# A pipelined transformer layer with eight experts: choice of experts behind the fourth transpose on VectorE, rank products behind the values, slot arithmetic on GpSimd, v ahead of q, the sums' transposes ahead of the next chunk

## What is computed

```
# block 0: base product + low-rank product (8 x 16 ranks, mixed by cond_8), then an fp8 product
u  = x @ W_base.T + b_base + 2 * sum_e cond_8[b,e] * (x @ As[e].T) @ Bs[e].T
x  = x + (fp8(bf16(u) / s_in) @ fp8(kernel / s_k)) * s_in * s_k + bias8
# block 1: z = x mixed by a weight of each sequence, then pre-norm attention, then one expert per token
z  = x @ (sum_g cond_8[b,g] * weight[g] * mask).T + bias
hn = layernorm(z);  q, k, v = hn @ wq + bq, hn @ wk + bk, hn @ wv + bv     # 16 heads of 8
z  = z + softmax(q k' / sqrt(8)) v @ wo + bo
hn2 = layernorm(z); idx = argmax(hn2 @ gate_w + gate_b)                    # 8 experts
x  = x + z + relu(hn2 @ w1[idx] + b1[idx]) @ w2[idx] + b2[idx]
```

## Time and profile before

| | us |
|---|---|
| median of 3 timed runs | 330.72 (330.45, 333.46, 330.72) |
| the profiled execution, its own time | 328.03 |
| span of the profiled execution | 326.2 |
| PE busy in the span | 257.6 (79%) |
| DVE busy | 211.4 (65%) |
| ACT busy | 194.9 (60%) |
| POOL busy | 198.3 (61%) |

### The profile page before, as it was taken

How to read it: one execution, slowest core, us unless ns; L and a number is a source line. 1 busy time by engine, 2 the same in 40 slices (tenths; PEclk the granted TensorE clock), 3 DMA queues, 4 the chain that set the end, 5 groups by cost and what they waited for, 6 DMA issues and landing times.

```text
span 326.2 us, 10489 instructions
## 1 busy us (share of the span) xinstructions
PE 257.6 (79%) x3558; PEld 197.4 (61%) x3565; DVE 211.4 (65%) x588; ACT 194.9 (60%) x422; POOL 198.3 (61%) x270
## 2 busy tenths in 40 slices
PE   3786979989799798798767574875994898999970
PEld 1454646756567567566554362354984787999970
DVE  4923698997979989889879558234252644656530
ACT  1578596986968969868837423033742344666640
POOL 1250572887887778866865538612866355787760
PEclk9999999999999999999795855559998799999995
DMA  6261101002010037010100100571532434333300
GB/s 211 99 219 73 34 3 34 3 34 67 3 67 32 0 113 324 32 36 2 46 24 2 67 3 0 138 222 49 155 110 79 128 103 120 89 97 90 96 22 0
DMA packets 13195, 24.65 MB, mean 76 GB/s; under 512 B 2636, under 2 KB 8784, under 8 KB 12896
## 3 DMA queue, kind: packets, MB, share of 16 engines
q1 hardware_dynamic: 9792, 17.26, 17.2%
q0 software_dynamic: 2784, 6.32, 5.7%
q10 hardware_dynamic: 576, 0.53, 0.5%
HBM read 16.60 MB, written 7.95 MB: 75 GB/s over the span
## 4 chain that ended last, share of the span: by engine, by line
PE 49%; DVE 21%; issue 11%; ACT 8%; POOL 3%; another core or an unknown queue 3%; DMA 2%; DVEq 1%; SPq 1%; POOLq 0%; ACTq 0%
PE so L735 7%; PE d L418 6%; PE d L430 6%; PE so L418 5%; PE so L430 5%; DVE mx L1163 4%; DVE pt L1181 4%; PE d L787 3%; DMA pack_sb<-pack 2%; PE d L760 2%; PE so L722 2%; PE d L775 2%; PE d L706 2%; POOL rs L1346 2%
## 5 line engine op out<-in xcount | busy, mean ns | idle before, releaser
L639 POOL DMA_INDIRECT out<-ob,rin x39 | 39.3, 1007 | 24.8 <-DVE w1s L564 11.1
L1419 POOL DMA_INDIRECT routed<-rows,slot x32 | 33.1, 1035 | 10.1 <-issue 10.1
L706 PE MATMUL d<-ybd,pack_sb 128*128 128x256 f32 x112 | 29.8, 396 | 0.0
L1353 POOL TENSOR_TENSOR t<-pr 128x512 f32<-128x512 f32 x16 | 20.5, 1281 | 13.2 <-ACT pr L959 13.2
L735 PE MATMUL so<-pt,v 32*32 32x128 f32 x1024 | 20.0, 295 | 10.4 <-DVE pt L1181 9.0
L418 PE MATMUL d<-xt,w1s 128*128 128x128 f32 x160 | 23.8, 294 | 3.3 <-issue 1.9
L430 PE MATMUL d<-pack_sb,mid 128*128 x160 | 24.0, 297 | 2.9 <-ACT mid L460 2.8
L1174 DVE SCALAR_TENSOR_TENSOR acc<-so,pack_sb,acc 128x512 f32<-128x512 f32 x24 | 17.9, 746 | 12.8 <-ACT acc L1065 12.1
L418 PE MATMUL so<-xt,w1s 128*128 128x128 f32 x152 | 21.7, 282 | 5.1 <-DVE ob L577 3.8
L430 PEld LDWEIGHTS d<-pack_sb,mid 128*128 128x128 f32 x160 | 21.1, 205 | 5.2 <-issue 5.2
L959 ACT ACTIVATE pr<-pr 128x512 f32<-128x512 f32 x32 | 20.0, 624 | 6.8 <-DVE pr L1167 6.7
(11 more groups left out here) (184 smaller groups left out, 665.2 us busy)
## 6 DMA issues: line engine op xcount, KB each, us to landing
rin<-routed SPq DMA_DIRECT2D x39, 128.5 KB
pack_sb<-pack SPq DMA_DIRECT2D x1, 2576.0 KB, 9.2
w1s<-w SPq DMA_DIRECT2D x8, 322.0 KB, 3.4
xb<-x_t SPq DMA_DIRECT2D x8, 256.0 KB, 3.5
pack_sb<-pack SPq DMA_DIRECT2D x1, 2048.0 KB, 8.3
routed<-pad SPq DMA_DIRECT2D x5, 128.5 KB
out<-ob,rin POOLq DMA_INDIRECT x39
pack_sb<-pack SPq DMA_DIRECT2D x1, 584.0 KB, 6.0
```

The costliest lines, as they stand in the source:

```text
L639: pool.indirect_dma_start(out, bass.IndirectOffsetOnAxis(rin[s % 8][:, 2 * H:ROW].bitcast(U32), 0), ob[u][:, :], None, bounds_check=N_TOK ...
L706: mm = pe.matmul(mix_bank(a, k)[:, u * 256:(u + 1) * 256], col[f"mix_w{k // 2}"][:, (blk % 4) * P:(blk % 4 + 1) * P], ybd[:, :, :].rearran ...
L1353: pool.tensor_tensor(t16[:, f, :], e32[:, :, 0:16], e32[:, :, 16:32], ALU.add).then_inc(sem["sums"], 1)
L1419: pool.indirect_dma_start(routed, bass.IndirectOffsetOnAxis(slot[:, g:g + 1], 0), rows[:, g, :], None).then_inc(sem["scattered"], 16)
```

## The change

It moves operations between places and engines and removes none of the results:

- DVE: in turns that have `j`, `pick` goes from between `shifted(2)` and `shifted(3)` to behind the fourth transpose, and `rank` from ahead of the fourth transpose to behind `eighth`.
- `place` leaves DVE. POOL does it with five small operations (a product, three adds of halves in place of one reduction, the cast) ahead of its scatters, with a semaphore `placed` of its own; `slot` now counts only the two operations of `rank`.
- POOL issues three of the four scatters, then `x1`, then the fourth.
- PE: the rank products go from ahead of wk to behind the values; wv, coded, wq in place of wq, coded, wv; the transposes of `rc` go ahead of `lora_a` of the next turn.
- ACT: `rc`, `v`, `qt`, then `yb`, `yb2` in place of `qt`, `rc`, `yb`, `yb2`, `v`.

```
@@ PE, start of a turn
+                if m is not None:
+                    wait(pe, "rcx", m + 1)
...
+                    for g in range(NG):
+                        mm = pe.transpose(turned_back(m)[:, g * P:(g + 1) * P],
+                                          rc[:, g * NH:(g + 1) * NH, :].rearrange("p h d -> p (h d)"), col["ident"])
+                    mm.then_inc(sem["rt_mm"], 1)
                 if a is not None:
                     wait_turn(pe, "x_in", a, p, 2)
                     wait(pe, "q_out", a - 1)
...
@@ PE, end of a turn
                     values(range(0, NG)).then_inc(sem["pv_mm"], 1)
...
+                if m is not None:
+                    wait(pe, "pick", 6 * (m + 1))
+                    pe.matmul(gates(m)[:, 64:64 + NG * E], upper_b[:, :], oh_b[:, :, :].rearrange("p g e -> p (g e)"),
+                              start=True, stop=False, skip_group_check=True)
...
+                    mm.then_inc(sem["rank_mm"], 1)
+                if late(m) and m == NC - 2:
+                    turn(0)
+                    hidden(0)
+                    turn(1)
                 if n is not None:
                     wait(pe, "x1_tok", n + 1)
...
+                if a is not None and not (isinstance(a, int) and a == 0):
+                    coded(a, n)
+                if n is not None:
+                    if m is not None:
+                        wait(pe, "slot", 2 * (m + 1))
+                    pe.matmul(dn[0][:, :], col["wq"], hn_t[:, :], start=True, stop=True).then_inc(sem["qkv_mm"], 1)
@@ ACT
-                if n is not None:
-                    wait(act, "qkv_mm", 3 * n + 2)
-                    act.activation(qt[:, :], dn[0][:, :], ACT.Identity, bias=col["bq"]).then_inc(sem["q_out"], 1)
                 if j is not None:
                     wait(act, "recip", j + 1)
...
+                if n is not None:
+                    wait(act, "qkv_mm", 3 * n + 2)
+                    wait(act, "pv_mm", n)
+                    act.activation(v[:, :, :], groups(dn[3][:, :]), ACT.Copy).then_inc(sem["v_out"], 1)
+                    wait(act, "qkv_mm", 3 * n + 3)
+                    act.activation(qt[:, :], dn[0][:, :], ACT.Identity, bias=col["bq"]).then_inc(sem["q_out"], 1)
@@ DVE
-                if m is not None:
+                if m is not None and j is None:
                     pick(m)
...
                     turned(j, 1)
                     turned(j, 2)
-                if m is not None:
-                    rank(m, p)
                 if j is not None:
                     turned(j, 3)
-                if m is not None:
-                    place(m)
+                if m is not None and j is not None:
+                    pick(m)
                 if early:
                     first_b()
                 if a is not None:
                     eighth(a)
                 if isinstance(a, int) and a == 1:
                     split_out_dve(dve)
+                if m is not None:
+                    rank(m, p)
@@ POOL
+            def place(m):
+                wait(pool, "slot", 2 * (m + 1))
+                hold(pool, "held_pool")
+                pool.tensor_tensor(pos[:, :, :], pos[:, :, :], oh_b[:, :, :], ALU.mult).then_inc(sem["placed"], 1)
...
+                pool.tensor_tensor(pos4[:, :, :], pos[:, :, 0:4], pos[:, :, 4:8], ALU.add).then_inc(sem["placed"], 1)
...
+                pool.tensor_tensor(pos2[:, :, :], pos4[:, :, 0:2], pos4[:, :, 2:4], ALU.add).then_inc(sem["placed"], 1)
...
+                pool.tensor_tensor(slot_f[:, :], pos2[:, :, 0], pos2[:, :, 1], ALU.add).then_inc(sem["placed"], 1)
...
+                pool.tensor_copy(slot[:, :], slot_f[:, :]).then_inc(sem["placed"], 1)
...
                 if m is not None:
+                    place(m)
                     wait(pool, "ids", m + 1)
                     wait(pool, "resid", m + 1)
-                    wait(pool, "slot", 5 * (m + 1))
+                    wait(pool, "placed", 5 * (m + 1))
                     wait(pool, "hn2", NG * (m + 1))
                     hold(pool, "held_pool")
-                    for g in range(NG):
...
+                    for g in range(NG - 1):
+                        scatter(g)
...
                     pool.tensor_tensor(x1[:, p, :], xb[:, p, :], yb2[:, :], ALU.add).then_inc(sem["x1"], 1)
+                if m is not None:
+                    scatter(NG - 1)
```

More of the change, by code:

```diff
@@ L877, in iteration @@
                     mm.then_inc(sem["hn_tr"], 1)
-                if m is not None:
-                    wait(pe, "pick", 6 * (m + 1))
-                    pe.matmul(gates(m)[:, 64:64 + NG * E], upper_b[:, :], oh_b[:, :, :].rearrange("p g e -> p (g e)"),
-                              start=True, stop=False, skip_group_check=True)
-                    for g in range(NG):
-                        mm = pe.matmul(gates(m)[:, 64 + (g + 1) * E:64 + (NG + 1) * E].rearrange("p (g e) -> p g e", e=E),
-                                       ones_b[:, :], oh_b[:, g, :].unsqueeze(1).to_broadcast([P, NG - g, E]),
-                                       start=False, stop=(g == NG - 1), skip_group_check=True)
-                    mm.then_inc(sem["rank_mm"], 1)
                 if late(m) and m == NC - 2:
@@ L910, in iteration @@
                     values(range(0, NG)).then_inc(sem["pv_mm"], 1)
-                    if late(m) and m == NC - 2:
-                        turn(0)
-                        hidden(0)
-                        turn(1)
-                if n is not None:
-                    if m is not None:
-                        wait(pe, "slot", 5 * m + 2)
-                    pe.matmul(dn[0][:, :], col["wq"], hn_t[:, :], start=True, stop=True).then_inc(sem["qkv_mm"], 1)
-                if a is not None and not (isinstance(a, int) and a == 0):
-                    coded(a, n)
+                if m is not None:
+                    wait(pe, "pick", 6 * (m + 1))
+                    pe.matmul(gates(m)[:, 64:64 + NG * E], upper_b[:, :], oh_b[:, :, :].rearrange("p g e -> p (g e)"),
+                              start=True, stop=False, skip_group_check=True)
+                    for g in range(NG):
+                        mm = pe.matmul(gates(m)[:, 64 + (g + 1) * E:64 + (NG + 1) * E].rearrange("p (g e) -> p g e", e=E),
+                                       ones_b[:, :], oh_b[:, g, :].unsqueeze(1).to_broadcast([P, NG - g, E]),
+                                       start=False, stop=(g == NG - 1), skip_group_check=True)
+                    mm.then_inc(sem["rank_mm"], 1)
[3 more added lines that the diff above has]
+                    turn(1)
                 if n is not None:
@@ L1080, in iteration @@
                     normed(1)
-                if n is not None:
-                    wait(act, "qkv_mm", 3 * n + 3)
-                    wait(act, "pv_mm", n)
-                    act.activation(v[:, :, :], groups(dn[3][:, :]), ACT.Copy).then_inc(sem["v_out"], 1)
             def between(act):
```

50 lines of the change are left out of this document (22 added, 28 removed).

## The result

The changed kernel takes **340.36 us** (median of 4 runs, 338.85 to 342.56) against 332.09 (4 runs, 330.45 to 333.81) of the kernel before beside it: a ratio of 1.0315, 95% interval 1.0255 to 1.0376. It is slower by 8.3 us, where +2.1 was forecast. The profiled execution took 341.0, span 339.2.

The account below looks back on a forecast made before the run. No engine is full; a turn is a ring of waits through several, ACT just behind DVE. Turn terms +1.0 +1.0 -0.4 +2.7 -0.3 -0.5 -1.4 gave +2.1 on a timed 330.72: 332.8 us, range 327.5 to 337.

Parts of the forecast that it names:

- The step that failed: POOL's list after the slots: three scatters, x1 in 1.11, fourth scatter 1.26, ybd 0.63, putting ybd at T' + 11.3.
- rival 1: Values' signal as late as 3.26, so slots at T' + 3.85 and 0.65 more per turn: 335.4 us; chance 0.25.
- Choice and rank off the path: DVE before the fourth transpose: 1.4 leaves the path, but ACT is next, so values gain only 0.43 a turn.
- The values' signal and `rank`: DVE behind the values: rank starts at T' + 2.9, slots there at T' + 3.2, bounds 2.75 and 3.85.
- lora_a: PE product waiting for ACT's qt behind rc and v: starts near T' + 6.0 instead of T + 4.14.
- POOL's arithmetic: Five dependent small operations making the slots on POOL: 1.45 in all, bounds 1.1 and 1.85.
- The mis-sized term: POOL between slots and first scatter: 0.17 of issue.
- Turns 1 to 3: Later qt costs +1.0 in turn 1 and +1.0 in turn 2; turn 3 gains 0.4.
- Turns 7 and 8: 1.4 taken off DVE counts: turn 7 -0.3; turn 8 -0.5, bounds +0.5 and -1.4.
- Turn 9: Values 2.5 sooner without pick's wait for the gate, then +1.1 behind them at half clock: sum -1.4.
- Rival 3: Shorter gaps in turns 8 and 9 keep PE at 2.4 GHz, saving up to 6: 326.8 us; chance 0.12.
- Rivals 2 and 4: POOL keeps its cover, signal early: 330.4, chance 0.15; choice brings whole 1.4 in seven turns: 321, chance 0.06.

Follow-up runs that it names:

- e13: The changed kernel unaltered, run again against the kernel before: 340.18 us, ratio 1.022.
- e14: The changed kernel with the 2.6 MB load also waiting until the scatters have landed, against the kernel before: 332.82 us, ratio of medians 1.003.
- e6: The kernel before with v ahead of q on PE and ACT and rc ahead of both, nothing else: 338.07 us, ratio 1.021.
- e4: The kernel before with only the slots' arithmetic moved from DVE to POOL, all four scatters ahead of x1: 330.03 us, ratio 1.027.
- e5: The kernel before with only the choice and rank products moved, slots' arithmetic staying on DVE behind rank: 332.20 us, ratio 0.997.
- e12: The kernel before unaltered, run against itself and profiled: 331.95 us, ratio 1.002.
- e9: The kernel before with the choice behind the fourth transpose in turn 9 alone: 318.43 us, ratio 0.997.
- e15: The kernel before with choice, v-first order and rc transposes moved, slots' arithmetic on DVE, four scatters ahead of x1: 333.85 us, ratio 1.004.
- e7: The kernel before with only the transposes of rc moved ahead of lora_a: 334.66 us, ratio 1.005.
- e16: The kernel before unaltered, run against itself once more: 331.83 us, ratio 0.992.
- e2: The kernel before with only the fourth scatter put behind x1: 326.71 us, ratio 1.017.
- e10: The kernel before with choice moved, place on DVE, fourth scatter behind x1, and the 2.6 MB load waiting for scatters: 329.25 us, ratio 1.026.
- e8: The kernel before with the choice behind the fourth transpose in turns 8 and 9 only: 319.79 us, ratio 1.001.

## Why the prediction was wrong, point by point

**The step that failed** is the one that went through POOL's list and moved the fourth scatter behind `x1`. I priced that scatter at 1.26 on POOL's own queue and went on to `ybd`. I did not ask who waits for its landing (ACT's `rows`, for the buffer) nor what `x1` releases besides PE (SP's load). "Three scatters, x1, the fourth" read as a gain of 1.26 for `x1`; it also sends a scatter through the DMA engines together with 2576 KB, once. No rival had it. It costs 7.4 us (e13 against e14) of the 8.4 between the two kernels on that chip; of the 9.9 that turn 6 is longer, 31.48 - 23.44 = 8.0 are the stall and 1.8 what the neighbouring turns lose too.

**Luck.** Without the stall the time is 332.8 on D, the forecast to the tenth, and that is chance: turns 3 to 8 are 10.4 longer there, where the sum had +1.5 for turns 3 to 8 (and +1.0 of turn 2 that falls into turn 3), and turn 9 with what follows is 10.8 shorter, where it had -1.4. On A the same kernel is 8.9 above the kernel before.

**Choice and rank off the path:** right. The fourth transpose starts 0.03 behind the fourth exponential (115.90 + 0.63, 116.56), ACT is next, and the values start 0.86 after that.

**The values' signal and `rank`:** `acc` began at T' + 2.13 with no wait, so the signal was there by then, and rival 1 (3.26) did not happen. `rank` started at T' + 2.6 and POOL had the slots at T' + 3.05, where I took 3.2. The 3.26 and 2.58 of the earlier trace rows were longer than the signal needed here; e6, which has no rank product behind the values, shows 3.28 again. What makes it early in the one and late in the other was not tried.

**lora_a:** T' + 5.65, I had 6.0. **POOL's arithmetic:** 120.47 to 121.96, 1.49 against 1.45. **The mis-sized term** is the time between the slots and the first scatter: 0.87 in the place of 0.17; e4 shows the same 0.87 without the rest of the change. It does not depend on which engine makes the slots, as e5 shows. The 0.17 of the earlier trace rows is POOL's pause behind work of its own: DVE's cast had ended at 112.51, 1.07 ahead of that scatter, so the time from cast to scatter was hidden. With it, and a first scatter of 1.12 for my 0.96, `mix(a, 0)` is at T' + 12.1 (I had 11.4), and turn 5 at 23.5 (22.75). The skill's rule that I weighed (GPSIMD Engine Reference of the Trainium skill, Key points: an SBUF interface shared with two-input VectorE instructions) agrees in direction: with `eighth` over, the first scatter fell from 1.37 to 1.12, though not to the 0.96 that I took.

**Turns 1 to 3.** In turn 1 wv started at 30.35 and the next `lora_a` at 33.45, 3.1 behind it, where the earlier trace rows have 2.0: +1.1 for +1.0. The values of turn 2 start 1.93 later, 0.85 of it there already when wv starts. Turn 3 is 0.36 longer; I had +1.0 and -0.4, that is 0.6.

**Turns 7 and 8:** -0.3 and -0.5 were predicted, +1.0 and +2.3 came (e14 less e12: +2.7 and +1.8). The late side in them is POOL's chain too: PE waits 0.50 for `x1` and 0.73 for `ybd` in turn 7 and 1.23 for `x1` in turn 8, and in both kernels with the whole change the two turns are over 24. I had let the 1.4 taken off DVE count there, though POOL's list was longer in the same turns.

**Turn 9:** 4.5 shorter, 2.5 predicted; and what I had as a loss behind it was a gain. I had charged the 8.16 from the start of the values to `acc` to half clock and kept it. PE's values of turn 9 and the window over them, changed kernel:

```profile
218.37 2.81 PE L737 MATMUL so<-pt,v 32*32 32x128 f32 x128 [1.34 <-DVE pt L1174]
```

```profile
218.37:221.20 2.83, 2.83 (x131) 2.21 (x132) 2.21 (x10) 0.00 (x0) 2.67 (x4) 0.50 0.03 6
```

and windows and PE's weight loads of the kernel before, with POOL's first scatter of the turn:

```profile
204.03:209.64 5.61, 5.20 (x99) 2.36 (x100) 2.11 (x9) 0.00 (x0) 4.20 (x6) 0.50 0.36 95
206.00:207.00 1.00, 0.89 (x11) 0.38 (x8) 0.35 (x1) 0.00 (x0) 0.70 (x2) 0.50 0.00 0
```

```profile
205.50 1.12 POOL L1419 DMA_INDIRECT routed<-rows,slot  x1 [0.41 <-issue]
206.06 0.21 PEld L735 LDWEIGHTS so<-pt,v 32*32 32x32 f32 x5 [0.45 <-issue]
206.83 0.18 PEld L735 LDWEIGHTS so<-pt,v 32*32 32x32 f32 x3 [0.56 <-issue]
```

At the same granted 0.50 the same 128 products take 2.81 us in the one, and in the other `acc` starts 8.16 behind their start. The clock was not the cause; in the kernel before the products come in handfuls, with half a microsecond of `issue` between their weight loads (time in which the profile shows nothing that the engine waits for). In e9, where only the choice of turn 9 is moved, they take 2.81 too. On D turn 9 is 6.1 shorter in e14 than in e12 and the rest behind it 4.7 (118.8 against 123.5), which pays for the 10.4 that turns 3 to 8 are longer. How much of the 4.7 is the values is not shown: e15 has them in 2.81 too, and its rest is 123.6.

What breaks the products up is open. It is not the load on the DMA engines alone: the handfuls begin at 206.06, and from 206 to 207 those engines are at 0.00. What the profiles have in common is the place of POOL's first scatter. Where it starts 1.5 to 1.9 behind the start of the values, and so among the products, they are chopped up on B, D, E and in the first profile (e6, e7, e12, e16: 8.0 to 8.2 to `acc`) and take 3.01 on A (e2). In all others it starts 3.4 or more behind it, after the last product, and they take 2.81. That was not tried by itself.

**Rival 3, the clock:** I had it as a gain behind turn 9. It acted as a loss in turn 6: 0.50 around and behind PE's wait of 4.2, though no engine had more work. The opposite case was in the text in one sentence, without a price. **Rivals 2 and 4:** POOL lost its cover, and the choice off DVE brought nothing in the loop.

**Open:** why the values of turn 9 run through on A and not on B, D and E, and what else makes the 3%; why turn 4 is longer than its neighbours in most variants, in some with `issue` in the scores (0.94 in e5, 1.06 in e10); why e5, whose turn 9 is 23.6, shows none of it in the total. For e8 and e9 on C the kernel before has no profile, so whether its turn 9 is 24.9 to 26.7 there, as elsewhere, is not known.

## What to carry to other kernels

When a transfer is moved in a list, follow it past its issue: who waits for its landing, and what else the operation now ahead of it releases on other queues; here a scatter issued together with a 2.5 MB load took 8 us instead of 3. Holding the large load back with one wait on a constant took back 7.4 us and left the new order untouched, so a collision is better mended at the transfer that nobody waits for yet. A pause read behind an engine's own earlier work is a lower bound, not the latency from the result it waits for: read that from the end of the producer, in a row where the consumer stood waiting. And a gain that rests on a slow place of the old kernel is only as large as that place is on the chip at hand.
